# Moving the start of TensorE's stationary operands within 256-byte SBUF rows, in an fp32r macaron transformer kernel

## The reference: what is computed

```python
x = x + 0.5 * ffn(layernorm(x), w_gate, w_up, w_down)      # hidden size 1024, silu(gate) * up
x = x + attn(layernorm(x), gamma, w_qkv, w_out)            # 16 heads of 64, 4 key/value heads, rotary, causal
x = x + 0.5 * ffn(layernorm(x), w_gate, w_up, w_down)
```

## Time and profile before

| | us |
|---|---|
| median of 3 runs | 579.34 (577.7 to 579.7) |
| the profiled execution | 579.26 |
| its span, first to last instruction | 577.5 |
| TensorE matmuls busy | 556.5 (96%) |
| TensorE weight loads busy | 528.7 (92%) |
| VectorE, ScalarE, GpSimd busy | 419.9, 379.5, 373.2 |

### The profile page before, as it was taken

How to read it: one execution, slowest core, us unless ns; L and a number is a source line. 1 busy time by engine, 2 the same in 40 slices (tenths; PEclk the granted TensorE clock), 3 DMA queues, 4 the chain that set the end, 5 groups by cost and what they waited for, 6 DMA issues and landing times.

```text
span 577.5 us, 13669 instructions
## 1 busy us (share of the span) xinstructions
PE 556.5 (96%) x4364; PEld 528.7 (92%) x4364; DVE 419.9 (73%) x1207; ACT 379.5 (66%) x1013; POOL 373.2 (65%) x410
## 2 busy tenths in 40 slices
PE   7779999999999999999999999999999999899997
PEld 4778999999999999999999999999999999789997
DVE  3686986859867695867867697767868698698533
ACT  4543893479836896379935897368934897479422
POOL 1645562886849775795839875697749877545322
PEclk9897999999999999999999999999999999999999
DMA  7340000250005200160004300070003400000001
GB/s 227 115 132 2 2 1 20 70 151 2 20 18 151 67 18 0 55 182 0 18 18 117 101 17 1 21 200 15 18 18 87 131 0 0 19 1 2 1 1 37
DMA packets 28090, 29.70 MB, mean 51 GB/s; under 512 B 2976, under 2 KB 25888, under 8 KB 28064
## 3 DMA queue, kind: packets, MB, share of 16 engines
q1 hardware_dynamic: 28064, 29.37, 18.3%
HBM read 8.39 MB, written 2.10 MB: 18 GB/s over the span
## 4 chain that ended last, share of the span: by engine, by line
PE 77%; DVE 7%; SPq 5%; issue 4%; ACT 2%; POOL 2%; DMA 2%; POOLq 0%; ACTq 0%; DVEq 0%
PE bank L979 51%; PE bank L988 9%; PE bank L1113 6%; PE bank L1083 5%; SPq L296 3%; PE bank L1108 3%; PE bank L1079 2%; SPq L285 2%; DVE hid L860 1%; DVE q_t L754 1%; ACT hid L602 1%; DMA q_t<-rotated 1%; DMA eye_sb<-in_eye 1%; POOL out_lo L342 1%; DVE qkv_lo L675 1%
## 5 line engine op out<-in xcount | busy, mean ns | idle before, releaser
L427 POOL TENSOR_TENSOR probs<-probs,inv_sum 128x512 f32<-128x512 f32 (+1 forms) x64 | 93.9, 1470 | 54.0 <-DVE inv_sum L828 53.9
L570 ACT ACTIVATE probs<-probs,neg_max 128x128 f32<-128x128 f32 (+1 forms) x256 | 113.2, 450 | 3.9 <-DVE neg_max L818 3.7
L436 POOL TENSOR_TENSOR hid_lo<-hid,hid_hi 128x512 fp32r<-128x512 f32 x64 | 82.8, 1298 | 33.7 <-ACT hid_hi L610 33.0
L979 PE MATMUL bank<-xf_t_hi,gate_hi 128*128 128x256 f32 x256 | 75.1, 293 | 6.9 <-DVE gate_lo L673 3.8
L979 PE MATMUL bank<-down_hi,hid_hi 128*128 128x256 f32 x256 | 72.9, 285 | 1.3 <-POOL hid_lo L436 1.2
L979 PE MATMUL bank<-xf_t_hi,up_hi 128*128 128x256 f32 x256 | 72.9, 285 | 0.0
L979 PE MATMUL bank<-down_hi,hid_lo 128*128 128x256 f32 x256 | 71.8, 280 | 0.0
L979 PE MATMUL bank<-xf_t_hi,up_lo 128*128 128x256 f32 x256 | 71.8, 280 | 0.0
L979 PE MATMUL bank<-down_lo,hid_hi 128*128 128x256 f32 x256 | 71.8, 280 | 0.0
L979 PE MATMUL bank<-xf_t_lo,up_hi 128*128 128x256 f32 x256 | 71.8, 280 | 0.0
L979 PE MATMUL bank<-xf_t_lo,gate_hi 128*128 128x256 f32 x256 | 71.6, 280 | 0.0
(11 more groups left out here) (142 smaller groups left out, 1809.3 us busy)
## 6 DMA issues: line engine op xcount, KB each, us to landing
q_t<-rotated SPq DMA_DIRECT2D x96, 128.0 KB, 2.6
k_t<-rotated_k SPq DMA_DIRECT2D x48, 128.0 KB, 2.6
x_in<-in_x SPq DMA_DIRECT2D x7, 256.0 KB, 2.7
out<-y_out SPq DMA_DIRECT2D x7, 256.0 KB, 2.1
probs<-in_w_qkv SPq DMA_DIRECT2D x4, 384.0 KB, 3.7
probs<-in_w_gate SPq DMA_DIRECT2D x2, 512.0 KB, 6.7
probs<-in_w_up SPq DMA_DIRECT2D x2, 512.0 KB, 7.6
probs<-in_w_down SPq DMA_DIRECT2D x2, 512.0 KB, 4.5
```

The costliest lines, as they stand in the source:

```text
L427: nc.gpsimd.tensor_tensor(part, part, inv_sum[:, slot].unsqueeze(2).broadcast_to([P, GROUP, keys]), ALU.mult).then_inc(p_done, 1)
L436: nc.gpsimd.tensor_tensor(hid_lo[:, slot].rearrange("p c n -> p (c n)"), hid[:, slot], hid_hi[:, slot].rearrange("p c n -> p (c n)").bitca ...
L570: last = nc.scalar.activation(part, part, ACT.Exp, bias=neg_max[:, slot, g:g + 1], scale=-1.0, accum_out=row_sum[:, slot, g:g + 1])
L979: last = nc.tensor.matmul(dst, a[x], b[y], start=start and i == 0, stop=stop and i == 2, skip_group_check=shared)
```

## The change

Two of the three unused tensors become longer. `before_weights` grows from 64 to 96 bytes and `before_stationary` from 128 to 192. No instruction, no operand's shape and no order changes.

```diff
-        sb("before_weights", [P, ROW // 4 // 4], align=ROW)
+        sb("before_weights", [P, 3 * ROW // 8 // 4], align=ROW)
...
-        sb("before_stationary", [P, ROW // 2 // 4], align=ROW)
+        sb("before_stationary", [P, 3 * ROW // 4 // 4], align=ROW)
```

## The result

| | before | after |
|---|---|---|
| median of 5 runs, us | 578.6 (577.32 to 579.7) | 584.35 (583.31 to 585.45) |
| ratio | | 1.010, 95% interval 1.0076 to 1.0123 |
| the profiled execution, us | 579.26 | 583.82 |
| its span | 577.5 | 582.0 |

The change makes the kernel 1% slower. The forecast was 578.2, a little faster than before; the kernel moved the other way. 584.35 lies inside the range (572 to 590) only because that range reached to the rival R2, on whose side it is.

What follows compares the result with a forecast made beforehand. TensorE's matmul stream, with steady paces of 113.3 and about 117.7 ns, was taken to bound the kernel. From 579.26 us only 1.1 us for the up-to-down step was subtracted, other terms zero, giving 578.2 us; range 572 to 590.

Steps and rivals of the forecast that it cites:

- R2: Rival: at 96 behind ordinary products have only the slow pace, 118 ns; +8.9 us, 588.2 us; chance 0.25.
- The bound and the resource: TensorE's matmul stream sets the time; layout acts only on how weight-load and moving-operand reads meet in SBUF.
- (1): Ordinary products go from 64 to 96 behind: between 113.3 and 117.7 ns a matmul, term put at zero.
- a mixture like today's: Central case for ordinary products at 96 behind: both paces remain, zero change; chance 0.37, range 575 to 582 us.
- (4): Restacking DMAs write q_t at 96 instead of 64: under 0.1 us each, TensorE seldom waits; put at zero.
- (2): Step from up or gate to down goes from 128 to 192 behind, down stays fast: 1.1 us saved.
- (3): Step from value_rows to gate stays at distance 0, where the slow pace begins today: zero.
- (5): Other engines' operands shift by 32 or 64 bytes; their slack hides any cost, so nothing in the sum.
- R4: Rival: layout does nothing, the two paces come from TensorE's own timing; 579.3 us, chance 0.06.
- R5: Rival: 96 behind also removes what holds the fast pace above 109 ns; 14 us less, 560 us, chance 0.02.
- R3: Rival: a third, slower pace of 122 ns a matmul; about 23 us more, 602 us, chance 0.05.

Runs made afterwards that it cites:

- e1_map: New kernel, TensorE alone streaming matmul bursts at 16 moving-to-stationary distances, 16 bytes apart: 113.33 ns a matmul at 64 behind, 118.4 to 118.8 at 96.
- e5_map_fine: Burst kernel of e1_map with distances at 4-byte resolution, plus burst pairs with one odd weight load between: 52, 64, 76 settle at 113.33 ns, 56 at about 118.
- e8_behind_128: Kernel before with weights at 128 and hidden and attention outputs at 256, so all ordinary products 128 behind: 586.25 us, ratio 1.0134.
- e4_only_stationary: Kernel before with only the second edit, hidden and attention outputs at 192, weights still at 64: 581.79 us, ratio 1.0036.
- e9_steps_down: Kernel before with down_w and out_w at 96, hidden and attention outputs at 160; distances stay 64, step up to down at 160: 579.84 us against 579.10.
- e2_shift32: Kernel before with operands moved by 32 bytes (weights at 96, moving at 32, outputs at 160), every distance kept: 579.66 us against 579.86, ratio 0.9999.
- e10_steps_all: As e9_steps_down, plus xa_t at 96 and qkv_w at 160, putting the value_rows to gate step at 160; against kernel before: 580.29 us, ratio 1.0022.

## Why the prediction was right or wrong

- **The bound and the resource**: right. The time moved with TensorE's pace, and e1_map shows the effect with all other engines idle.
- **(1), the distance of the ordinary products**: this is the step that failed. I took "a mixture like today's" because the same products show both paces at one distance. That shows that distance is not the only thing that chooses a pace at 64. It does not show that every distance offers both. The bursts show that it does not: at 96 behind none of six went below 117.2 ns. The term was put at zero, and the kernel grew by 5.75 us. The nearest rows pointed the right way, with a slow step at 128 and a neighbour only 32 bytes off, but that they did was partly luck. The right choice was R2 or a wide split without a centre: at 4 bytes' resolution fast and slow distances alternate (e5_map_fine), so no interpolation between measured distances could have settled it.
- **R2's mechanism and its price**: the sign and the place were right (the fast stretch now reads 118 ns), the size was too high: 588.2 forecast, 584.35 measured, +8.9 against +5.75 us. The slow pace of 118 was right. The term that was mis-sized is the share that reaches the end. I took 95%. By the starts, the 256-column steps of a turn without a wait rose from 115.1 to 118.0 ns, 440 x 2.9 = 1.3 us, just what R2 has for a turn; but a turn grew by 0.56 us. The rest is taken back at TensorE's waits. Over an ordinary step, the steps with a wait in them held 2.6 us a turn before and 1.8 after. More than half of that difference, 0.44 us, lies at one place, where `down` is followed by `scores` (L1079). Before, TensorE's waits in the stretch of the five turns have this row
```profile
PE bank L1079 <- DMA q_t<-rotated: 1.5, 4, 0.6
```
  and those after have no such row. One of these places, first before, then after:
```profile
325.17 0.28 PE L979 MATMUL bank<-down_hi,hid_lo 128*128 128x256 f32 x1
325.56 0.50 PE L1079 MATMUL bank<-k_t,q_t 128*128 128x256 f32 x2
```
```profile
327.73 0.28 PE L979 MATMUL bank<-down_hi,hid_lo 128*128 128x256 f32 x1
327.84 0.40 PE L1079 MATMUL bank<-k_t,q_t 128*128 128x256 f32 x2
```
  Before, TensorE arrived early and stood 0.39 us from start to start; after, it arrives later in its turn and goes on in 0.11. Such steps number six in five turns before and two after. The profile puts four of the six down to the restacked queries, so the DMAs of term (4), which had TensorE wait for them only "a few times a turn" and at no price, are part of what hid R2's cost. A smaller share lies at the waits for the activation. In before and after alike a `gate` group is followed by `up`, and the next `gate` waits for tanh and product of the first; the chain goes by that way and not by `up`. After:
```profile
312.75 1.70 PE bank L979 x12
...
314.55 0.61 ACT hid L602
315.18 0.70 DVE hid L860
...
315.93 1.67 PE bank L979 x12
```
  From one `gate` start to the next it is 3.18 us, against 3.13 before (310.42 to 313.55, the pair behind the steps 309.04 and 309.68 of the earlier trace rows). 24 matmuls lie in it, and only the 12 of `gate` add to it; `up` is slower inside the wait. e8_behind_128 agrees: its waits hold 1.8 us like those after, so nothing more is taken back, and there the further rise of the step arrives whole.
- **(2), the step from `up` to `down`**: wrong in its rule and worth nothing. In the pairs a step at 192 brings the slow pace. e4_only_stationary has that step in the kernel, but `down` behind it is then 128 behind and slow anyway. That such a step starts a slow `down` group, at 128, was right (e5_map_fine, e9_steps_down), but removing it in e9_steps_down gave no time back.
- **(3)**: right that the step at 0 starts the slow pace in the kernel (five turns of five before); it had no role any more, since 96 behind has no fast pace to lose.
- **(4) and (5)**: right that neither costs anything. e2_shift32 puts `q_t` at 96 with no effect (ratio 0.9999); the busy times of the other engines moved by 0.1%. What (4) missed is only that the wait for these DMAs could shrink, as said above.
- **R4**, and the sentence of the Trainium skill beside it ("TensorE: Matmul & The Clock Gate", "Step-by-step: what each phase is for"), by which loading weights takes no read bandwidth from the running matmul: the runs speak against it for fp32r operands, 113.3 ns at 64 behind against 118.4 at 96 with nothing else changed in the stream. **R5** did not occur: at 256 columns no burst went below 113.3 ns, at 96 behind or elsewhere. **R3** did not occur: no distance held 122 ns over a burst but 48 behind from a gap (123.3), and that one read 117.8 behind transposes.

## What to carry to other kernels

Where TensorE is the bound and every matmul loads new weights, the place of the stationary against the moving operand within 256 bytes is a parameter, worth 0.7 to 1.3% of this kernel. Measure it in bursts of a few dozen matmuls on an idle core, all distances in one kernel and each more than once, since neighbouring distances say nothing of each other and one distance can have two paces. Read the pace from start to start. Then look for the waits that can take the difference back before you price it: here a turn had 0.8 us of them to give, so of the first 1.3 us a turn 0.56 arrived and of the next 0.4 all. And check a whole-kernel mixture by timing it: rules for single steps did not add up.

## What the runs showed of the hardware

- An fp32r stream of 256-column matmuls, each with its own weight load, never went below 113.33 ns a matmul, and settles between that and 123.3 ns by the distance between the two operands: 113.33 at 64 behind, 116.7 at 208, 118.4 to 118.8 at 96, 120.0 at 0 and 144 (e1_map). Moving both operands by 32 bytes makes no difference to the kernel (e2_shift32, ratio 0.9999).
- At 64 and 192 behind two paces are stable, 113.33 and 117.78 ns. In single bursts one odd weight load switches between them, in either direction (e5_map_fine); in the kernel a step at 128 brings the slow pace between `up` and `down` in five turns of five and one at 160 in none. Behind transposes the rule fails: with the step at 160 `projection` is slow there in four turns of five (e9_steps_down) and `qk` in five of five (e10_steps_all). Why is open.
- 512-column matmuls prefer another distance: 226.67 ns at 0 behind, 228.9 at 192, 233 to 234.4 at 64, 96 and 128, while 256 columns at 0 behind take 120.0.
- Fast distances can lie 12 bytes apart (52, 64, 76) with places at 118 to 120 ns (56 to 60, 68 to 72) between them. Why is open.
- That the pattern repeats every 256 bytes was assumed and not tested by itself. The two tiles of one distance lie 1,280 bytes apart in e1_map, and both settled at 113.33 ns at 64 behind.
